# Two mixers, cross attention and a mixture of experts on one core: rows sent home by token, one convolution moved, loads issued before barriers

## The reference

```python
x = x + mamba0(layernorm(x))            # RMS norm, 512 channels, 16 states, causal conv of 4 taps
x = x + xattn0(layernorm(x), ctx)       # 16 heads over 1601 context rows, then an MLP
x = x + moe0(layernorm(x))              # below
x = x + mamba1(layernorm(x))
x = x + xattn1(layernorm(x), ctx)       # causal, 512 context rows
x = x + moe1(layernorm(x))              # top 2 of 8, and a shared expert

def moe0(x):                            # top 1 of 8, at most 512 tokens per expert
    f = x @ W_proj + b_proj; r = softmax(f @ W_gate)
    w, e = top1(r); w = w / w           # as the reference has it
    for each expert: h = gelu(ln1(f[tok] @ W1 + b1)); o = h @ W2 + b2
    out[tok] += o * w                   # tokens beyond the 512 keep a row of zeros
    return layernorm(out) * ln_g + ln_b
```

## Time and profile before

| | |
|---|---|
| three runs | 2909.48, 2915.48, 2918.29 us; median 2915.48 |
| profiled execution | time 2914.07 us, span 2912.2 us |
| busy, share of span | TensorE 83%, VectorE 75%, ScalarE 50%, GpSimd 31% |
| mean granted TensorE clock | 0.91 |
| barriers 0, 3 and 4 passed at | 555.8, 1609.4, 2144.7 |

### The profile page before, as it was taken

The page is one execution under the profiler, slowest core; times in us unless marked ns, Lnnn a source line. Parts: engine busy times, 40 slices in busy tenths (PEclk is TensorE's granted clock), DMA queues, the critical chain, the costliest instruction groups (busy, mean ns, idle before and its releaser), DMA issues.

```text
span 2912.2 us, 31513 instructions
## 1 busy us (share of the span) xinstructions
PE 2417.0 (83%) x10888; PEld 1575.3 (54%) x10888; DVE 2194.8 (75%) x3180; ACT 1444.4 (50%) x2547; POOL 894.5 (31%) x617
## 2 busy tenths in 40 slices
PE   4989886588998899947993698988668888899998
PEld 1333332266776565736993233343234443799998
DVE  4999999688997365336995599999956653567776
ACT  5666564254665222213673565656412445356663
POOL 2868776300000000020002377877611235100004
PEclk7999999899999799978997699999987887889999
DMA  4031130380000000023331303203054231246652
GB/s 171 1 116 55 62 117 0 118 288 23 23 1 1 35 1 1 0 89 112 110 129 44 139 4 112 98 19 117 0 81 94 51 100 59 86 149 218 218 207 91
DMA packets 99065, 243.12 MB, mean 83 GB/s; under 512 B 9182, under 2 KB 63339, under 8 KB 91740
## 3 DMA queue, kind: packets, MB, share of 16 engines
q1 hardware_dynamic: 82540, 216.20, 22.7%
q10 hardware_dynamic: 11760, 12.32, 1.6%
q0 software_dynamic: 4608, 12.59, 1.4%
HBM read 187.93 MB, written 46.66 MB: 81 GB/s over the span
## 4 chain that ended last, share of the span: by engine, by line
PE 49%; DVE 28%; ACT 10%; issue 8%; POOL 2%; DMA 1%; ACTq 0%; DVEq 0%; SPq 0%; POOLq 0%
DVE psum L635 11%; PE psum L109 6%; PE psum L111 6%; PE psum L432 6%; PE psum L110 6%; PE psum L116 3%; DVE ch L643 3%; PE psum L397 3%; ACT WH L3119 2%; PE psum L1265 2%; PE psum L1279 2%; ACT g L3266 2%; PE psum L1249 2%; PE psum L2575 1%; PE psum L1227 1%
## 5 line engine op out<-in xcount | busy, mean ns | idle before, releaser
L317 POOL TENSOR_TENSOR bu<-u,row 128x1024 f32<-128x1024 f32 x254 | 597.0, 2355 | 289.0 <-DVE psum L635 190.9
L432 PE MATMUL psum<-ch,ident 128*128 128x512 f32 x1024 | 510.1, 627 | 137.9 <-DVE ch L643 137.3
L635 DVE TENSOR_TENSOR_SCAN psum<-psum,bu 128x1024 f32<-128x1024 f32 x256 | 585.5, 2287 | 18.8 <-ACT psum L514 18.6
L432 PEld LDWEIGHTS psum<-ch,ident 128*128 128x128 f32 x1024 | 188.5, 196 | 426.7 <-DVE ch L643 245.0
L514 ACT ACTIVATE psum<-dt,A 128x511 f32<-128x511 f32 x512 | 332.4, 682 | 0.4
L643 DVE TENSOR_TENSOR ch<-psum,row 128x1024 f32<-128x1024 f32 x256 | 313.0, 1223 | 7.6
L1535 POOL IOTA i<- 128x128 f32 x1 | 0.3, 345 | 710.2 <-DVEq L3411 710.2
L397 PE MATMUL psum<-hT,inw 128*128 128x512 f32 x256 | 140.7, 682 | 42.8 <-ACT sz L474 27.3
L3266 ACT ACTIVATE g<-psum,bias 128x256 f32<-128x256 f32 x248 | 101.2, 470 | 133.7 <-PE psum L111 126.0
L109 PE MATMUL psum<-WH,hs 128*128 128x256 f32 x496 | 145.3, 293 | 4.7 <-DVE hs L3346 2.3
L109 PE MATMUL psum<-xT,WH 128*128 128x256 f32 x496 | 142.3, 287 | 7.6 <-DVE xT L3309 7.6
(11 more groups left out here) (403 smaller groups left out, 5907.6 us busy)
## 6 DMA issues: line engine op xcount, KB each, us to landing
W<-in_m1W SPq DMA_DIRECT2D x24, 2052.0 KB, 8.6
row<-Ascr SPq DMA_DIRECT2D x64, 512.0 KB, 4.8
row<-Bscr SPq DMA_DIRECT2D x64, 512.0 KB, 4.8
m1buf<-zt SPq DMA_DIRECT2D x8, 2048.0 KB, 16.7
...
```

What stands on the lines that cost most here:

```text
L317: e.tensor_tensor(m.bu[i % 3][:, :, :], u, m.row[:, g, 0, :, :], ALU.mult).then_inc(*m.fed.up)
L432: p = pe.matmul(m.y, k.ident, m.ch[i % RING_C][:, j, :], start=False, stop=g == UNITS - 1 and j == 1)
L635: dve.tensor_tensor_scan(flat, flat, m.bu[i % 3][:, :, :].rearrange("p a n -> p (a n)"), 0.0, ALU.mult, ALU.add).then_inc(*m.scan.up)
```

## The change

Three parts are merged.

*Rows by token.* The weight w and the token's home are written as columns 256 and 257 of each row sent to `m0buf` (1032 bytes). For each expert GpSimd takes them from `xe` (`tags`). The final layer norm is applied per expert to `ob`: since LN(w o) = w (o - mean)/sqrt(w^2 var + eps), VectorE takes statistics of `ob` (`out_stats`), GpSimd, ScalarE (`out_dev`) and VectorE (`out_inverse`) form scale and shift, ScalarE applies them to expert e-1 (`out_rows`) in the body of e, and GpSimd sends the rows to their token's place in `m0res` (`out_home`, four indirect DMAs per expert). For the last expert VectorE does it. `m0res` is cleared in advance, by token. ln_b is added to x by VectorE in the last expert's body. Two of the four normalisations of the hidden rows go from VectorE to ScalarE. Mixer 1 then loads the rows by token into `row`, which is free at its start (`mamba_home`), and VectorE multiplies by ln_g (now in `zt`), adds to x and takes the statistics: batch 0 at the opening, batches 1 to 3 behind its convolutions; their square roots are in ScalarE's unit 1, their reciprocals in VectorE's unit 4. SP writes B and C after the last of these adds.

*Convolution.* In both mixers, batch 0's fourth convolution is made by TensorE with the diagonals, like those of later batches; ScalarE draws it ahead of the third Silu.

*Loads.* Keys' wk (to the tile of wq), its first 384 context rows and two rows of ln1 are issued before barrier 0, once the last batch of mixer 0 has its dt and z; wk and the first context of cross attention 1 before barrier 4; the weights of mixer 1 in the body of expert 2. Tiles are placed anew for that. `m0buf` is cleared by 2 DMAs instead of 16.

```diff
-FIRST = [("h", 0), ("h", 1)] + [("in", i) for i in range(4)] + [("xp", 0)] + [("dt", i) for i in range(4)]
+FIRST = [("h", 0), ("h", 1)] + [("in", i) for i in range(4)] + [("conv", 3), ("xp", 0)] + [("dt", i) for i in range(4)]
...
+def mamba_weights_sp(k, m, sp):
...
+
+
+def mamba_home(m, b):
+
+    return m.row[:, b, 0, :, :].rearrange("p a (t c) -> p (a t) c", c=D)
+
+
+def mamba_sp(k, m, sp):
+    if m.rnd:
+        for b in range(B):
+            sp.dma_start(mamba_home(m, b), k.DR["m0res"][T * b:T * b + T, :].rearrange("(t p) c -> p t c", p=128)).then_inc(*m.home_in[b].up)
+        sp.wait_ge(*m.home(B - 1))
+    else:
+        mamba_weights_sp(k, m, sp)
     for b in range(B):
         sp.wait_ge(*m.drawn(mamba_use("xp", b, 0)))
...
+
+
+def mamba_prepared_sp(k, m, sp):
+
+    sp.wait_ge(*m.drawn(mamba_use("z", B - 1, 3)))
+    sp.wait_ge(*m.dt_in(4 * B - 1))
...
     elif w == "conv":
+        if b == 0:
+            pe.wait_ge(*m.diag(0))
+            pe.wait_ge(*m.drawn(mamba_use("in", 0, j)))
         for f in range(4):
             p = pe.matmul(bank, m.dg[:, 4 * (j - 1) + f, :], m.xs[:, j, f:f + T], start=f == 0, stop=f == 3)
...
-        if b == 0 or j == 0:
+        if b == 0 and j == 2:
+            mamba_item_act(k, m, act, "conv", 0, 3)
+        if j == 0 or b == 0 and j < 3:
             act.wait_ge(*m.conv(conv_at(b, j)))
         else:
             act.wait_ge(*m.drawn(mamba_use("conv", b, j)))
...
+    if m.rnd:
+        x_stats_act(k, act, 4 * m.rnd)
     mamba_item_act(k, m, act, "h", 0, 0)
...
+        if m.rnd and i == 1:
+            for j in range(1, B):
+                x_stats_act(k, act, 4 * m.rnd + j)
         if n == 6 and b:
...
+def mamba_home_dve(k, m, dve, b):
+
+    x, rows = k.X[:, 4 * b:4 * b + 4, :], mamba_home(m, b)
+    dve.wait_ge(*m.home_in[b](0))
+    dve.tensor_tensor(rows, rows, k.zt[:, 0:1, :].to_broadcast([128, 4, D]), ALU.mult).then_inc(*m.times.up)
+    dve.wait_ge(*m.times(b))
+    dve.tensor_tensor(x, x, rows, ALU.add).then_inc(*m.home.up)
+    dve.wait_ge(*m.home(b))
+    x_stats_dve(k, dve, 4 * m.rnd + b)
+
+
 def mamba_dve(k, m, dve):
-    for b in range(B if m.rnd else 1):
-        dve.wait_ge(*k.inv_dev(4 * m.rnd + b))
+    if m.rnd:
+        mamba_home_dve(k, m, dve, 0)
+        x_inverse_dve(k, dve, 4 * m.rnd)
+    dve.wait_ge(*k.inv_dev(4 * m.rnd))
...
-    for ob in range(4):
+    for ob in range(3):
         mamba_conv_dve(k, m, dve, ob)
+    if m.rnd:
+        for j in range(1, B):
+            mamba_home_dve(k, m, dve, j)
...
+        if m.rnd and i == 4:
+            for j in range(1, B):
+                x_inverse_dve(k, dve, 4 * m.rnd + j)
         if n == 5 and b + 1 < B:
+            if m.rnd:
+                dve.wait_ge(*k.inv_dev(4 * m.rnd + b + 1))
             mamba_rows_dve(k, m, dve, b + 1)
...
+def keys_first_sp(k, m, sp):
+
+    sp.dma_start(m.wq[:, :, :], k.d["x0wk"]).then_inc(*m.w_k.up)
+    sp.dma_start(m.cx[0][:, 0:3, :], k.d["ctx"][0, 0:384, :].rearrange("(t p) c -> p t c", p=128)).then_inc(*m.ctx_first.up)
+    for n in ("ln1_g", "ln1_b"):
+        sp.dma_start(m.vec[n][:, :], row_of(k, "x0" + n, D)).then_inc(*m.ln_in.up)
+
...
-    for j in range(TRASH // 256):
-        sp.dma_start(k.DR["m0buf"][256 * j:256 * j + 256, :].rearrange("(t p) c -> p t c", p=128), k.zt[:, :, :]) \
+    wider = k.zt[:, :, :].rearrange("p a c -> p (a c)")[:, 0:D + 2].unsqueeze(1).to_broadcast([128, 16, D + 2])
+    for j in range(TRASH // 2048):
+        sp.dma_start(k.DR["m0buf"][2048 * j:2048 * j + 2048, :].rearrange("(t p) c -> p t c", p=128), wider) \
             .then_inc(*k.cleared["m0"].up)
...
-    sp.dma_start(k.DR["m0res"][TRASH:TRASH + 1, :], k.zt[0:1, 0, :]).then_inc(*k.cleared["m0"].up)
+    sp.dma_start(k.DR["m0res"][0:N, :].rearrange("(t p) c -> p t c", p=128), k.zt[:, 0:1, :].to_broadcast([128, NT, D])) \
+        .then_inc(*k.cleared["m0"].up)
...
         if e:
             sp.wait_ge(*m.c_at(e - 1))
+            sp.wait_ge(*m.tagged(e - 1))
         sp.dma_start(m.xe[:, :, :], k.DR["m0buf"][CAP * e:CAP * e + CAP, :].rearrange("(t p) c -> p t c", p=128)).then_inc(*m.xe_in.up)
 
-    for n in ("ln_g", "ln_b"):
-        sp.dma_start(m.vec[n][:, :], row_of(k, "m0" + n, D)).then_inc(*m.vecs.up)
+    sp.dma_start(m.ln_b[:, :], row_of(k, "m0ln_b", D)).then_inc(*m.vecs.up)
+
+    sp.wait_ge(*k.cleared["m0"](TRASH // 2048))
+    sp.wait_ge(*k.cleared["m1"](E))
+    sp.dma_start(k.zt[:, 0, :], row_of(k, "m0ln_g", D)).then_inc(*m.vecs.up)
...
+        if e == 2:
+
+            mamba_weights_sp(k, following, sp)
+    for home in m.home:
+        sp.wait_ge(*home(2 * E - 1))
...
-    pool.wait_ge(*m.get(0))
-    pool.wait_ge(*m.sent(NT - 1))
-    for i in range(2):
-        pool.wait_ge(*m.stored[i](E // 2 - 1))
-    for t in range(NT):
-        pool.indirect_dma_start(m.XF[:, t, :], None, k.DR["m0res"], bass.IndirectOffsetOnAxis(ap=m.get_i[:, t:t + 1], axis=0)) \
-            .then_inc(*m.back[t // 4].up)
...
+    def tags(e):
+        pool.wait_ge(*m.xe_in(e))
+        if e == 0:
+            pool.wait_ge(*m.rooms(0))
+        pool.tensor_tensor(m.tf[:, e, :], m.room[:, e, :], m.xe[:, :, D + 1], ALU.add).then_inc(*m.tf_in.up)
+        pool.tensor_copy(m.tw[:, e, :], m.xe[:, :, D])
+        pool.tensor_tensor(m.t2[:, e, :], m.xe[:, :, D], m.xe[:, :, D], ALU.mult)
+        pool.tensor_scalar(m.tn[:, e, :], m.xe[:, :, D], -1.0, None, ALU.mult)
+        pool.wait_ge(*m.tf_in(e))
+        pool.tensor_copy(m.ti[:, e, :], m.tf[:, e, :]).then_inc(*m.tagged.up)
...
+    def out_var(e):
+        pool.wait_ge(*m.tagged(e))
+        pool.wait_ge(*m.o_mv(e))
+        if e:
+            pool.wait_ge(*m.o_sc(e - 1))
+        pool.tensor_tensor(m.osd[:, :], m.omv[e % 2][:, :, 1], m.t2[:, e, :], ALU.mult).then_inc(*m.o_var.up)
+
+    def out_scale(e):
+        pool.wait_ge(*m.o_rec(e))
+        pool.tensor_tensor(m.nsc[:, :], m.osd[:, :], m.tn[:, e, :], ALU.mult).then_inc(*m.o_neg.up)
+        if e:
+            pool.wait_ge(*m.o_n(e - 1))
+        pool.tensor_tensor(m.osc[:, :], m.osd[:, :], m.tw[:, e, :], ALU.mult)
+        pool.wait_ge(*m.o_neg(e))
+        pool.tensor_tensor(m.onb[:, :], m.nsc[:, :], m.omv[e % 2][:, :, 0], ALU.mult).then_inc(*m.o_sc.up)
+
+    def out_home(e, t):
+        pool.indirect_dma_start(k.DR["m0res"], bass.IndirectOffsetOnAxis(ap=m.ti[:, e, t:t + 1], axis=0), m.ob[e % 2][:, t, :], None) \
+            .then_inc(*m.home[e % 2].up)
+
+    tags(0)
+    tags(1)
+    for e in range(E):
+        if e + 2 < E:
+            tags(e + 2)
+        if e:
+            out_scale(e - 1)
+            pool.wait_ge(*m.o_n(e - 1))
+            for t in range(4):
+                out_home(e - 1, t)
+        if e + 1 < E:
+            out_var(e)
+    for t in range(4):
+        pool.wait_ge(*m.o_last(t))
+        out_home(E - 1, t)
 
...
+        act.wait_ge(*m.h_nb(e))
+        for t in (2, 3):
+            h = m.hN[e % 2][:, t, :]
+            a = act.activation(h, h, ACT.Identity, scale=m.hrs[e % 2][:, t:t + 1], bias=m.hnb[e % 2][:, t:t + 1])
+        a.then_inc(*m.h_na.up)
+
+    def out_dev(e):
+        act.wait_ge(*m.o_var(e))
+        act.activation(m.osd[:, :], m.osd[:, :], ACT.Sqrt, bias=k.eps).then_inc(*m.o_sd.up)
+
+    def out_rows(e):
+        act.wait_ge(*m.o_sc(e))
+        for t in range(4):
+            o = m.ob[e % 2][:, t, :]
+            a = act.activation(o, o, ACT.Identity, scale=m.osc[:, t:t + 1], bias=m.onb[:, t:t + 1])
+        a.then_inc(*m.o_n.up)
 
...
+        if e:
+            out_dev(e - 1)
         if e + 1 < E:
             hidden_norm(e + 1)
         if e + 2 < E:
             first_split(e + 2)
+        if e:
+            out_rows(e - 1)
         if e + 1 < E:
             for t in range(4):
                 own.use()
...
-        act.wait_ge(*m.o_in(4 * e + 3))
-        act.dma_start(k.DR["m0res"][CAP * e:CAP * e + CAP, :].rearrange("(t p) c -> p t c", p=128), m.ob[e % 2][:, :, :]) \
-            .then_inc(*m.stored[e % 2].up)
...
+        dve.scalar_tensor_tensor(out=m.hnb[e % 2][:, :], in0=mv[:, :, 0], scalar=-1.0, in1=m.hrs[e % 2][:, :], op0=ALU.mult, op1=ALU.mult) \
+            .then_inc(*m.h_nb.up)
+        for t in range(2):
+            normed(dve, hN[:, t, :], hN[:, t, :], mv, m.hrs[e % 2], t).then_inc(*m.h_n.up)
+
+    def out_stats(e):
+        seen = []
         for t in range(4):
-            normed(dve, hN[:, t, :], hN[:, t, :], mv, m.hrs[e % 2], t).then_inc(*m.h_n.up)
+            dve.wait_ge(*m.o_in(4 * e + t))
+            dve.bn_stats(m.ost[:, t, :], m.ob[e % 2][:, t, :]).then_inc(*v.up)
+            seen.append(v.last())
+        for t in range(4):
+            dve.wait_ge(*seen[t])
+            a = dve.bn_aggr(m.omv[e % 2][:, t, :], m.ost[:, t, :])
+        a.then_inc(*m.o_mv.up)
+
+    def out_inverse(e):
+        dve.wait_ge(*m.o_sd(e))
+        dve.reciprocal(m.osd[:, :], m.osd[:, :]).then_inc(*m.o_rec.up)
 
     dve.wait_ge(*m.iotas(0))
...
+            if e + 1 == E and o % 2:
```

(56 more changed lines are left out.)

167 lines of the change are left out of this document (63 added, 104 removed).

## The result

The changed kernel takes 2882.86 us (median of four runs, 2874.02 to 2883.48) against 2916.75 of the kernel before: ratio 0.9883, 95% interval 0.9861 to 0.9905. The forecast was 2880, its range 2869 to 2893. Two later groups of runs, in which the kernel before took 2929.7 and 2934.3 us, gave 2900.57 and 2892.86 for the changed kernel: ratios 0.9900 (0.9882 to 0.9918) and 0.9868 (0.9842 to 0.9895). The ratio repeats; the time itself lay in the forecast's range in two of the three groups, in the last at its upper end.

A forecast was written before the change was run, and what follows sets the result against it. TensorE was taken to bound the expert loop, the chain of waits the other touched stretches. Seven terms sum to -35.4 us, taking the profiled execution from 2914.07 to 2878.7; 1.4 more for the median gives 2880, range 2869 to 2893.

The forecast's parts named there:

- Part 1: First mixer's opening: fourth convolution on TensorE lets the xpw projection start at 38.25 instead of 40.45; -2.2 us.
- Part 2: Loads ahead of the first barrier: the keys' cast starts 5 us sooner and the rest follows; -5.0 us.
- part 7: Loads ahead of barrier 4: TensorE no longer waits 3.86 for cT; -4.0 us.
- Part 3: Routing: two short VectorE operations more, and rows of 1032 instead of 1024 bytes; +0.4 us.
- Part 4: Expert loop: ScalarE normalises before casting W1, so VectorE's split waits; pitch +1.1 an expert, +5 us in all.
- the 0.6 ahead of the adds: Tail: ln_b's add and a reciprocal behind ScalarE's root push the last expert's output adds back by 0.6 us.
- Rivals A: Expert loop paced by ScalarE and VectorE: bodies 0 to 6 each pay 2.5 us, 17.5 instead of 5; 2892 us; 14%.
- C: Expert loop stays TensorE's: its term is 0; 2875 us, or 2871 with a better opening; 18%.
- Part 5: Tail: gathers and weighting go; eight GpSimd sends 1.27 apart bound it, the last landing 2.40 later; -34.5 us.
- rival B: Tail, slow sends: the last eight take 2.46 each instead of 0.96, +12 against 0.6; 2891 us; 10%.
- Part 6: Second mixer's opening: dt add +2.4, ScalarE's table loads +1.9, three reciprocals among the scans +0.6; +4.9 us.
- the sum that counted 1.28: Whole-kernel total with 1.28 us per table load, 2880; with the skill's 2.66 per switch it would be 2883.

The follow-up runs named there:

- roots later: Changed kernel with mixer B's three roots moved to ScalarE's unit 4, reciprocals to VectorE's unit 5: 2889.06 us, ratio 0.9863 to the kernel before (2934.30).
- conv on VectorE: Changed kernel with batch 0's fourth convolution back on VectorE in both mixers: 2882.72 us, ratio 0.9888 to the kernel before (2915.27).
- rows of 6 early: Changed kernel with expert 6's root, scales, rows and sends moved into expert 7's body: 2889.04 us, ratio 0.9863 to the kernel before (2929.73).
- before again: The kernel before, unedited, profiled a second time; its median in that group of runs is 2915.27 us.
- cast first: Changed kernel with ScalarE casting the next W1 ahead of its two normalised hidden tiles: 2889.31 us, ratio 0.9874 to the kernel before (2929.73).
- changed, third: The changed kernel unedited, run a third time: 2892.86 us, ratio 0.9868 to the kernel before (2934.30).
- late loads: Changed kernel with the early loads issued behind barriers 0 and 4 again: 2906.05 us, ratio 0.9924 to the kernel before (2929.73).
- changed again: The changed kernel unedited, run a second time: 2900.57 us, ratio 0.9900 to the kernel before (2929.73).
- three edits: Changed kernel with W1 cast before normalising, expert 6's rows in expert 7's body, no GpSimd drain at barrier 3: 2890.29 us, ratio 0.9861 (before 2934.30).
- five edits: W1 cast first, expert 6's rows early, no drain, plus mixer B: SP's wait behind write, roots at unit 4, projections between diagonals: 2876.53 us, ratio 0.9808 (before 2934.30).
- no drain: Changed kernel with GpSimd signalling barrier 3 by a small memset instead of a drain: 2882.73 us, ratio 0.9884 to the kernel before (2915.27).
- write first: Changed kernel with SP waiting for the last join behind its write of B and C: 2887.84 us, ratio 0.9906 to the kernel before (2915.27).

## Why the prediction was right, point by point

**Part 1 (-2.2, measured -1.4).** The mechanism held: from the first convolution on, the projection started 2.3 earlier. The step mis-sized is what came behind it: I let its duration stand at 5.44, and it took 6.48. The 5.44 of the earlier trace rows was itself a mixture, half of it at the lower clock level; as the product moved ahead, the clock didn't rise as much earlier, and two more matmuls fell on the lower level. TensorE had stood 9.2 us ahead of it, and 15.9 in the kernel before.

**Part 2 (-5.0) and part 7 (-4.0)** measured -5.0 and -4.3, and undoing them gave back 5.0 and 4.1. These are the cleanest terms, because the chain of waits named the transfer as the only thing between the barrier and TensorE.

**Part 3 (+0.4)** measured -0.1: the wider rows were covered.

**Part 4 (+5, with the 0.6 ahead of the adds +5.6)** measured +5.85. The pitch rose by 0.86 against 1.1, and the cause is the one given, order at ScalarE and not load: the cast ahead of the normalising took all but 0.5 of it back. Rivals A (2.5 a body) and C (nothing) fall.

**Part 5 (-34.5, measured -32.1 counted the same way: -32.7 and the 0.6).** The sends were GpSimd-bound as forecast, and 0.96 each: VectorE was through, so rival B didn't come. (It is real in the bodies, where GpSimd has time: beside VectorE's W2 splits, with both operands in SBUF, a send took 1.46 to 2.61.) What failed is the last step, "lands 2.40 later". I took the landing of the last row as the end of the stage; the barrier wanted GpSimd's drain, and passed 5.06 behind the last send's start. The 2.5 between is what the version without the drain gave back, and is the whole miss. In the kernel before, three rounds of VectorE's work lay behind the gathers and hid it: GpSimd's drain ended at 1589.4 there, 20 us ahead of the barrier. The cost was uncovered, not made, by the change.

**Part 6 (+4.9, measured +5.4).** The opening followed the forecast to 0.8 us at every event up to GpSimd's product. The first scan itself came 3.8 later than before, where the dt add is 2.6 later; by the fifth scan it is 4.1, against the 4.3 forecast up to there. The three reciprocals took 0.28 instead of 0.6. And 0.9 is a cost I had not counted: VectorE's rows for batch 1 took 4.28 (four tiles, beside two GpSimd products), 3.39 in the kernel before (3.40 where the roots come later), and 1.38 where GpSimd does nothing. The Trainium skill, SBUF — State Buffer, section SBUF: two separate sides, has an exclusive lock between the two engines for such pairs of instructions; by that rule VectorE waits for the product under way before its next instruction, and the trace agrees in direction (2.0 us more beside one product, 2.9 beside two). The table loads took 1.28 each, the first of the rows above with 0.02 ahead of and behind it; the 2.66 with a drain that the Trainium skill gives (ScalarE: Activation LUTs, section What ACT_TABLE_LOAD costs) isn't seen here, and the sum that counted 1.28 was the better one.

**The stretches without a term (-4.25, +1.88, +4.10).** They cancelled nearly, so the total came out 3 us from the forecast while single stretches missed by 4. That is luck: the same kernel's end came out 13 to 14 us longer in its other two profiles. Cut once more behind x1, at VectorE's 84th operation from the end, the stretch falls in two, with the mean granted clock of each:

| version, group | x1 to cut, clock | cut to end, clock |
|---|---|---|
| roots later, c | 694.1, 0.880 | 75.0, 0.954 |
| conv on VectorE, b | 697.3, 0.873 | 62.3, 0.965 |
| rows of 6 early, a | 699.1, 0.868 | 75.2, 0.952 |
| before | 700.8, 0.873 | 62.4, 0.965 |
| before again, b | 700.8, 0.870 | 62.3, 0.965 |
| cast first, a | 702.8, 0.864 | 75.1, 0.926 |
| changed | 705.0, 0.857 | 62.3, 0.960 |
| changed, third, c | 705.0, 0.857 | 75.2, 0.905 |
| late loads, a | 705.5, 0.863 | 75.2, 0.926 |
| changed again, a | 706.3, 0.857 | 75.1, 0.927 |
| three edits, c | 706.7, 0.855 | 76.3, 0.925 |
| five edits, c | 709.2, 0.856 | 74.7, 0.932 |
| no drain, b | 712.5, 0.849 | 62.3, 0.960 |
| write first, b | 717.6, 0.836 | 62.2, 0.961 |

In the first part the length goes with the clock over all 14 profiles, but for 2 or 3 us: TensorE's low level (1.2 GHz) falls on more or fewer of its products from one execution to the next. In the changed kernel's first profile one such stretch lies between 2236 and 2266, in cross attention 1; in its second profile the clock there is 0.98 and another stretch lies 100 us later. Changed versions lie on both sides of the kernel before, so the +4.1 can't be called the change's.

The second part has two lengths, and the group decides which: 62.2 to 62.4 in the first group and b, 74.7 to 76.3 in a and c. The clock is lower there, but in the third profile of the changed kernel two waits, 5.9 of VectorE and 4.9 of ScalarE, also stand there whose end the trace puts down to nothing that it knows. Why those groups are 13 us longer stays open.

In the loops the mean clock doesn't tell the length: loop A has 0.96 at 480.3 and at 476.0. The lengths come in steps. Loop A is 476.03 to 476.07 in seven of the twelve changed versions, 476.9 to 478.8 in the other five, and 480.2 and 480.3 before. The difference before to after is made of VectorE's waits for TensorE's sum ahead of a gate: five before (0.44, 1.13, 0.87, 0.69, 1.55), one in the first profile after (0.64), 4.0 of the 4.25. The other lengths come from waits at mostly the same places. Ahead of one of them, the 50th scan, before and five edits wait (1.13, 0.88), changed and changed again don't. From 35 to 25 us ahead of it the granted clock was 0.83 in the first two and 1.00 in the others, and over the last 36 us TensorE had no idle time in the first two, 2.3 and 2.6 us in the others. That fits the low level falling at a bad place, but no run holds the clock fixed, so it is argued only, and why no changed version has the 480.2 of before stays open. Mixer B's loop is 439.85 before, and 439.85 to 439.87 in three changed versions too (cast first, no drain, five edits): its +1.88 isn't the change's doing.
